# A slab's own keys copied to PSUM, and read there as the broadcast operand of VectorE's comparisons

## The reference, cut to what matters

```python
def reference(x, src, dst, ...):
    edge_index = jnp.stack([src, dst])
    x = _layernorm(x + _L0_gnn_ref(x, ..., edge_index))   # 3 rounds of segment_sum(m[src], dst) and a GRU cell
    x = _layernorm(x + _L1_gnn_ref(x, edge_index, ...))   # hypergraph convolution, batch norm, relu
    x = _layernorm(x + _L2_gnn_ref(x, edge_index, ...))   # attention by source, segment softmax
    x = _layernorm(x + _L3_gnn_ref(x, edge_index, ...))   # MLP on every edge, segment_sum, MLP on the nodes
    return x
```

## Time and profile before

| | us |
|---|---|
| median of 3 runs | 4950.32 (4942.99 to 4955.18) |
| the profiled execution | 4954.31 |
| its span, first to last instruction | 4952.6 |
| TensorE busy | 3939.9 (80%) |
| VectorE busy | 3227.2 (65%) |
| ScalarE busy | 2297.8 (46%) |
| GpSimd busy | 1747.1 (35%) |

### The profile page before, as it was taken

One profiled execution on the slowest core, in us unless ns is written; L12 is line 12 of the kernel. 1 busy time (PEld: TensorE's weight loads), 2 busy tenths in 40 slices (PEclk: granted clock), 3 DMA queues, 4 the chain that ended last, 5 costly groups with the idle time before them and its releaser, 6 DMA issues. The chain is left out here.

```text
span 4952.6 us, 80614 instructions
## 1 busy us (share of the span) xinstructions
PE 3939.9 (80%) x23797; PEld 3319.9 (67%) x23798; DVE 3227.2 (65%) x7668; ACT 2297.8 (46%) x3163; POOL 1747.1 (35%) x1769
## 2 busy tenths in 40 slices
PE   5888139968889989977989987999996666555667
PEld 4665128757778768766867866999996665555565
DVE  7777539858788788776664446788775444444444
ACT  0001126535555555535555556888874333333333
POOL 3777777776000000000000000000005777777772
PEclk8999569989999999998999997999997666787667
DMA  9900039969278548817877851455433333333331
GB/s 371 362 27 3 1 123 371 329 223 318 83 268 285 192 161 294 274 47 240 295 210 274 295 176 32 141 149 149 139 114 116 102 102 102 102 103 106 103 102 48
DMA packets 318864, 858.38 MB, mean 173 GB/s; under 512 B 84767, under 2 KB 109073, under 8 KB 318603
## 3 DMA queue, kind: packets, MB, share of 16 engines
q1 hardware_dynamic: 205964, 619.48, 38.3%
q10 hardware_dynamic: 57185, 177.25, 9.5%
q0 software_dynamic: 55456, 58.46, 4.7%
HBM read 669.98 MB, written 185.03 MB: 173 GB/s over the span
## 5 line engine op out<-in xcount | busy, mean ns | idle before, releaser
L925 POOL DMA_INDIRECT big<-table,idx_ring x880 | 854.1, 971 | 2785.3 <-ACT idx_ring L943 2517.5
L1433 POOL DMA_INDIRECT adj_t<-cell_val,cell_at x832 | 858.2, 1031 | 320.3 <-issue 320.3
L765 PE MATMUL ps<-tiles_r,stage_r 128*128 128x512 f32 x2028 | 806.6, 398 | 30.1 <-ACT tiles_r L714 24.7
L991 PE MATMUL ps<-big,stage 128*128 x1760 | 400.0, 419 | 312.2 <-DVE onehot L1003 156.7
L991 PEld LDWEIGHTS ps<-big,stage 128*128 128x128 f32 x1760 | 370.1, 320 | 333.6 <-issue 333.5
L635 DVE TENSOR_SCALAR_CACHE_REDUCE big<-ps 128x512 f16<-128x512 f16 (+2 forms) x724 | 429.6, 652 | 124.1 <-PE ps L587 115.2
L714 ACT CAST tiles_r<-onehot 128x1024 fp32r<-128x1024 f16 x338 | 354.9, 1050 | 291.3 <-PE ps L767 154.7
L772 PE MATMUL ps<-stage,big 128*128 128x130 f32 x4046 | 468.2, 278 | 18.3 <-DVE big L875 15.5
L772 PEld LDWEIGHTS ps<-stage,big 128*128 128x128 f32 x4046 | 463.8, 194 | 19.0 <-issue 15.2
L965 ACT ACTIVATE stage<-stage 128x512 f32<-128x512 f32 x220 | 138.4, 629 | 727.2 <-DVE stage L1018 727.2
L765 PEld LDWEIGHTS ps<-tiles_r,stage_r 128*128 128x128 f32 x2028 | 387.5, 191 | 122.7 <-issue 25.8
(11 more groups left out here) (428 smaller groups left out, 7601.9 us busy)
## 6 DMA issues: line engine op xcount, KB each, us to landing
onehot<-adj_t SPq DMA_DIRECT2D x332, 512.0 KB
big<-adj_t SPq DMA_DIRECT2D x332, 512.0 KB
onehot<-adj_s SPq DMA_DIRECT2D x170, 512.0 KB
adj_t<-rows ACTq DMA_DIRECT2D x13, 6656.0 KB, 50.8
adj_s<-big ACTq DMA_DIRECT2D x157, 512.0 KB
stage<-local_rows SPq DMA_DIRECT2D x110, 512.0 KB, 3.8
big<-adj_s SPq DMA_DIRECT2D x84, 512.0 KB
x_fm<-adj_s SPq DMA_DIRECT2D x84, 512.0 KB
```

What stands on the lines that cost most here:

```text
L765: nc.tensor.matmul(psum_fm(p, n)[:, 0:cut], upper_rows[:, k, :], tile[:, 0:cut], start=k == 0, stop=False, skip_group_check=True)
L925: nc.gpsimd.indirect_dma_start(row_ring[slot][:, u, :], None, table[0:N, :], bass.IndirectOffsetOnAxis(idx_ring[:, slot * CH + u:slot * CH ...
L991: last = nc.tensor.matmul(ps[:, 4 + 2 * h + g, (u % 4) * P:(u % 4 + 1) * P], ring_ohT[:, h * CH + u, :], q_nm[:, bass.ds(blk[u] * P, P)], ...
L1433: nc.gpsimd.indirect_dma_start(out, bass.IndirectOffsetOnAxis(cells[:, c:c + 1], 0), cell_val[:, c:c + 1], None).then_inc(S(name), 16)
```

## The change

`halo(n)` gets a second copy behind the first: the slab's own 104 keys go from `keyx` to 104 free columns of PSUM bank 3 (128 to 231 for even slabs, 232 to 335 for odd ones), and DVE waits for both copies. The comparisons take their broadcast operand from there. Their other operand stays in SBUF, as do the output, the shapes, the number of comparisons and all semaphores between engines.

```diff
             def halo(n):
                 dve.wait_ge(S("halo_given"), n + 1)
                 nc.vector.tensor_copy(keyx[:, n, SLW:KEYS], ps[:, n % 2, 0:HALO]).then_inc(S("halo_kept"), 1)
+                nc.vector.tensor_copy(own_keys(n), keyx[:, n, 0:SLW]).then_inc(S("own_kept"), 1)
                 dve.wait_ge(S("halo_kept"), n + 1)
+                dve.wait_ge(S("own_kept"), n + 1)
...
+            def own_keys(n):
+                return ps[:, 3, P + n % 2 * SLW:P + (n % 2 + 1) * SLW]
...
                     wait(dve, S("same_used"), done - 3)
-                    own = keyx[:, n, 0:SLW]
                     behind = keyx[:, n, SHIFTS * r + 1:SHIFTS * r + 1 + SLW]
-                    nc.vector.tensor_tensor(eq[done % 4], own.unsqueeze(1).to_broadcast([P, SHIFTS, SLW]),
+                    nc.vector.tensor_tensor(eq[done % 4], own_keys(n).unsqueeze(1).to_broadcast([P, SHIFTS, SLW]),
                                             bass.AP(behind.tensor, behind.offset, [behind.ap[0], [1, SHIFTS], [1, SLW]]),
                                             ALU.is_equal).then_inc(S("same_ready"), 1)
```

## The result

| | before | changed |
|---|---|---|
| median, us | 4951.54 (4942.99 to 4955.18, 4 runs) | 4899.99 (4897.28 to 4904.94, 4 runs) |
| span of the profiled execution, us | 4952.6 | 4903.2 |

The ratio is 0.9902, with a 95% interval from 0.989 to 0.9913: the median is 51.6 us lower, where 51.3 were forecast.

What follows compares the result with a forecast made beforehand. GpSimd's scatter queue was taken to bound the stage. Freed scatters −51.6 and the copy +0.25 gave −51.3 us on a median of 4950.3, so 4899.0 us, range 4888 to 4925, chance 0.84.

Steps and rivals of the forecast that it cites:

- What bounds the stage: Between 83 and 700 us the program waits for GpSimd's queue of scatters; VectorE is far ahead from slab 1 on.
- What is held, and by what: A comparison with two SBUF operands blocks GpSimd's scatter for its whole length; one PSUM and one SBUF operand don't.
- The fixed part: VectorE's 120 cycles for a PSUM source against 58 for SBUF would lengthen a comparison by 65 ns; forecast unchanged.
- shows no wait with one: Reading of the trace before: VectorE instructions with only one SBUF input, such as lines 385 and 1018, stretch no GpSimd instruction.
- Freed scatters: 235 scatters beside the comparisons, 104 to 453 us, lose their blocking: 51.6 us less ahead of line 1469, bounds 0 to 51.6.
- The copy: New 104-element copy into PSUM with its wait, in slab 0 ahead of the first scatter: +0.25 us, bounds 0 to 0.5.
- What is late next: Line 1469, issued at 626.2, waits for `pairs_ready` at 576.6; 48 us remain, so no other gate takes over.
- Carried whole: Matrix pass: its remaining 416 scatters and its loads start as much earlier, distances unchanged, so the whole gain reaches the end.
- Nothing is freed: Rival at the comparisons: the moving operand in SBUF alone still blocks the scatters; 4950.6 us, chance 0.07.
- half comes back: Rival: until 259.3 us zeroing fills the DMA engines and 44% of the gain is not won; 4921.7 us, chance 0.06.
- The slower rival: Rival at the comparisons: repeated PSUM read at half rate, 2.91 us each; +163 us, 5113 us, chance 0.03.
- break-even: VectorE 101 us later at line 1469, 0.53 us per comparison beyond PSUM-independent pace of PE, decides against the change.

Runs made afterwards that it cites:

- The pair with VectorE later: Changed kernel with 150 or 400 small memsets on VectorE ahead of the block counts; 4899.98 us and 4956.02 us.
- copy alone: Changed kernel with its second copy and wait, but comparisons reading both operands from SBUF as before; 4953.59 us, ratio 1.0011 to the kernel before.
- other operand: Against the changed kernel, roles exchanged: whole row of 392 keys copied to PSUM, moving operand read there, own keys in SBUF; 4901.81 us.
- other slot: Changed kernel with the comparison's two operands in exchanged slots, SBUF first and PSUM second; 4904.64 us, ratio 0.9912 to the kernel before.
- half the slabs: Changed kernel with slabs 0 to 3 comparing against PSUM, slabs 4 to 7 against SBUF as before; 4928.51 us, ratio 0.9962 to the kernel before.
- the changed kernel's repetition: The changed kernel, unaltered, timed again together with the edge-stage edit; 6199.16 us, against 6124.52 for the kernel before.
- halves: Kernel before, both operands in SBUF, no copy, each comparison cut into two of 624 elements; 6118.34 us against 6124.52 for the kernel before.
- the moved gathers: Changed kernel with 8 scatters and 7 gathers of lines 1465 and 1469 moved 24 scatters earlier or later in GpSimd's queue; 4904.15 and 4903.55 us.
- the edge stage: Changed kernel with line 1003's comparison run as 8 instructions with one SBUF tensor, pointer scalar and accumulator output; 6177.87 us, repeated 6170.27.
- the first series: Copy alone, other operand, other slot and half the slabs, timed together with the kernel before; that kernel took 4949.08 us.
- the third: Halves, the edge stage and the changed kernel's repetition, timed together with the kernel before; that kernel took 6124.52 us.

## Why the prediction was right

**What bounds the stage** was right: GpSimd's queue. The pair with VectorE later shows both sides of it: 38.8 us on VectorE cost nothing, 53.5 us of waiting on GpSimd cost 52.

**What is held, and by what** was right for the comparison, and is now shown rather than inferred from lines 385 and 1018: copy alone, other operand, other slot, half the slabs each did what the number of SBUF operands says. In the kernel before, 164 of the 170 scatters over 1 us between 120 and 453 us end 0.78 to 0.88 us behind a comparison's end; in the changed kernel none does. The rule of the Trainium skill (SBUF — State Buffer, Who interferes with whom) agrees in every one of these runs. The fixed part that it gives for a PSUM source (VectorE: DVE Perf Modes, The TRN2 errata) does not show: 1453 and 1451 ns with a PSUM operand against 1453 without.

The prediction went too far in one reading, that this trace "shows no wait with one" SBUF operand. Two SBUF operands are enough to hold a scatter, but they are not needed. Line 2384 reads one SBUF tensor, without an accumulator, and the scatter beside it ends at 641.09, 0.85 us behind it:

```profile
639.61 0.63 DVE L2384 TENSOR_SCALAR acc<-acc 128x896 int32<-128x896 int32 x1 [5.10 <-DMA acc<-edges,pair_idx]
...
639.71 1.38 POOL L1433 DMA_INDIRECT adj_t<-cell_val,cell_at  x1 [0.30 <-issue]
```

The kernel before has the same pair (line 2380 at 687.84 for 0.63 us, a scatter at 687.97 for 1.35), and lines 2158, 2160, 2236, 2321, 2351 and 2390 of the changed kernel, with one SBUF tensor each, hold one scatter each in the same way. All seven take 0.69 to 0.78 ns for each element, where the comparison takes 1.16. Beside line 2327, with one SBUF tensor and an accumulator output and 1.29 ns for each element, none of the 40 scatters from 520 to 570 us takes over 0.98 us. The forecast didn't depend on this, since such instructions are few and the change leaves them as they are.

**The terms of the sum.**
- Freed scatters: forecast −51.6; the queue between the first scatter and line 1469 shortened by 49.7 us. The window of 104 to 453 us isn't all comparisons. At its head VectorE prepares slabs 1 to 7 with instructions that the change leaves as they are, two of them with two SBUF operands and a cast with one, and each holds up a scatter. The first of the three:

```profile
108.44 0.92 DVE L2231 TENSOR_TENSOR big<-big,slab_f 128x728 f32<-128x728 f32 x1
...
108.70 1.49 POOL L1433 DMA_INDIRECT adj_t<-cell_val,cell_at  x1 [0.30 <-issue]
```

  The three scatters take 1.49, 1.60 and 1.22 us where the median is 0.967: 1.4 of the 1.9 us too many. The rest is the price of a free scatter: 152.03/158 = 0.962 counts scatters that the window's ends cut, and whole ones take 0.967 us there too.
- The copy: forecast +0.25. The new copy takes 0.26 us in the trace, and from the first copy's start to the first comparison's it is 0.74 instead of 0.49 us: +0.25. The first scatter nevertheless came 1.44 us later, 86.94 against 85.50. Of that 0.2 us lie ahead of the change (line 2142 starts at 19.87 instead of 19.67) and 1.0 us in slab 0's first two loop turns on TensorE, 120 matmuls in 12.75 instead of 11.77 us. The eleven traces with a PSUM operand in slab 0 began between 85.66 (slots exchanged) and 86.94, among them the changed kernel's repetition at 85.73; those with both operands in SBUF began at 85.50, 86.47 (copy alone) and 86.58 (halves). That spread is the run's, not the change's.
- What is late next: nothing, as forecast. The 48 us of slack were 50.4: `pairs_ready` at 579.2, line 1469 at 629.6, and 38.8 us of added lateness passed.
- Carried whole: right in size, and the reason given was half of it. The prediction let both the pass's start and its scatters move; the moved gathers show that the start is worth nothing within 30 us, which leaves the scatters' end to carry the gain.

**Sum against measurement.** −51.3 forecast, −49.4 in the spans of the two profiled executions, −51.6 in the medians. The two differ by less than the runs of one kernel do, so that the medians meet the forecast to 0.3 us is luck; the terms say 49.4.

**The rivals.** "Nothing is freed" and "half comes back" fell with the windows above, the second also with the half dose: 0.971 us under full traffic. The slower rival's mechanism, a repeated PSUM read at half rate, did not occur. Its break-even in VectorE's lateness was confirmed (102.5 us against 101). Its remark that comparisons of up to 1.80 us cost almost nothing leaves out slab 0, whose 24 comparisons lie ahead of the first scatter: 0.25 us each would put that off by some 6 us. No run has slower comparisons.

## What to carry to other kernels

When GpSimd's indirect DMAs are the bound, look at the durations of single ones beside VectorE's instructions. If they end a fixed time behind an instruction with two SBUF operands (here 0.84 us), put one of the operands into free PSUM columns, whichever operand and slot is handy. A form with one SBUF tensor, a pointer scalar and an accumulator output held up nothing here either; one SBUF tensor alone is no guarantee, as line 2384 shows. All this pays though VectorE gains nothing. Before moving work within such a queue, ask whether the next stage hangs on its first input or its last: 61 us between two starts of the matrix pass made no difference, because its last input came no sooner or later.

## What the runs showed that was not expected

In the two series with the halves and the edge stage, TensorE sat idle for its own instructions. The group of its matmuls of line 1795, in the changed kernel's first trace and in its repetition there (busy, mean, idle before):

```profile
L1795 PE MATMUL ps<-big,ident_h 128*128 128x104 bf16 (+1 forms) x2880 | 319.2, 248 | 9.3 <-issue 8.7 <-DVE big L2184 0.6
```

```profile
L1795 PE MATMUL ps<-big,ident_h 128*128 128x104 bf16 (+1 forms) x2880 | 360.7, 257 | 461.9 <-issue 461.0 <-DVE big L2184 0.5
```

In the windows looked at it goes with the stretches in which GpSimd issues indirect DMAs. Two windows of the repetition, all engines (PE, PEld, DVE, ACT, POOL, then clock, DMA share and GB/s), beside the scatters and in the matrix passes after them:

```profile
104.00:453.00 349.00, 112.18 (x801) 70.34 (x802) 90.85 (x109) 1.28 (x1) 192.71 (x199) 0.61 0.43 159
1700.00:2400.00 700.00, 661.89 (x4629) 530.56 (x4627) 602.19 (x1837) 420.75 (x372) 0.00 (x0) 0.98 0.81 291
```

From 28 to 85 us, ahead of the first scatter, TensorE gets 390 matmuls done (386 in the first trace), and from 1700 to 2400 us it is busy 95% of the time; beside the scatters it gets 801 done in 349 us instead of 2623. The edge stage's gathers, too, spread over 1479 us instead of 1123. Under that condition the changed kernel was slower than the kernel before of the same series, 6199.16 against 6124.52 us (ratio 1.0112, 1.0092 to 1.0132). VectorE, held back by TensorE, is then what GpSimd waits for (205.8 us at line 1465 alone), so freed scatters have nothing to shorten there. Why it is slower rather than equal, and what brings the condition about, no run here settles. The chip alone does not: the first series, at 4900 to 4950 us, ran on the same chip as the third.
